# One fp32 product of an LSTM pipeline with 7 block products for 8, and two residual sums moved to GpSimd

## The chip, the cores and the metric

The kernel runs on one core of a Trainium2 chip. The metric is device time in microseconds (us) of one execution, the median of several runs. PE is the TensorE matmul queue, PEld its weight load, DVE is VectorE, ACT is ScalarE, POOL is GpSimd, SP is SyncE.

## What is computed

A batch of 16 sequences, 512 steps, width 512: an LSTM with a residual sum, then a plain tanh RNN over its result with another residual sum. All is fp32.

```python
def step(carry, xw_t):                      # LSTM; xW = x @ Wx0 + b0, Wx0 is 512 x 2048
    prev_h, prev_c = carry
    a = xw_t + prev_h @ Wh
    i, f, o = (sigmoid(a[:, j*512:(j+1)*512]) for j in range(3))
    g = tanh(a[:, 1536:])
    next_c = f * prev_c + i * g
    next_h = o * jnp.tanh(next_c)
...
def step(h, xw_t):                          # RNN; xW = y0 @ Wx1 + b1, Wx1 is 512 x 512
    h_next = jnp.tanh(h @ Wh + xw_t)
...
x = x + LSTM(x)      # y0
x = x + RNN(x)       # y1
```

## The kernel before

**Layout.** Features lie on the 128 partitions. A width of 512 is four slices k. An output column block of 32 features goes to one quarter q of the PE array, so every product is issued as groups of four matmuls (`tiles`, L175), one for each quarter, that run side by side; the small matrix of states or inputs (32 columns) is the loaded one, the weights stream through. The LSTM's 2048 gate columns are 512 columns for each quarter, cut in two halves of 256, each with the four gates of half of the features.

**The input product** x*Wx0 is taken for two steps at once (PAIR, 2 x 16 batch rows). `input0(p, half)` (L191) issues two of the four slices: two groups of four fp32 matmuls with 512 columns, into `in0_ps`. ScalarE writes the bias there first (`bias0`, L468) and later copies the sum, one half after the other, into the banks of the recurrent product (`seed0`, L480), with a mask that picks the rows of the step. `rec0_ps` has two banks for each of the two halves, by the parity of the step.

**The recurrent product** `recurrent0(t)` (L206) adds h*Wh0 with h and Wh0 each in two fp16 parts: 64 matmuls with 256 columns, half 0 first. Its first matmul waits for `h0_ready[0]`, the third slice for `h0_ready[1]`.

**The cell.** VectorE turns the half (`turn0`, L350), adds the two partial sums (`add0`), ScalarE takes the tanh of the gates, VectorE does `gate_products`, `cell`, `state_high` (two instructions, L381 and L382) and `state_low` (L389, which posts `h0_ready`). `add_y0` (L392) and `add_y1` (L420) are the residual sums. Step t of the LSTM and step s = t - 4 of the RNN share an iteration (`turn1`, `add1`, `state1_high`, `state1_low`).

**Order.** Every engine's queue is written out by hand, one loop over t for each engine. PE's order in an iteration: recurrent0(t), half an input0, half an input1 (y0*Wx1, fp32, 128 columns), recurrent1(s). VectorE's order stands in L428 to L461, ScalarE's in L537 to L565. GpSimd has only memsets, an iota and the two maxima over the partitions (L170) by which the weights are scaled. The maximum for the RNN's weights is asked for in iteration 1 and read by VectorE in iteration 2 (`split_rnn_weights`).

## Time and profile before

| | before |
|---|---|
| median of 3 runs | 2290.19 us (2289.34 to 2290.5) |
| the profiled execution's own time | 2287.48 us |
| its span | 2285.6 us |
| PE busy | 2242.9 us, 98% |
| DVE busy | 1974.7 us, 86% |
| ACT busy | 1642.1 us, 72% |
| POOL busy | 1.8 us |
| TensorE clock | granted 0.998 of full |

The trace's timeline gives the start and length of each instruction; neighbours on one engine overlap by their pipelines, so what counts is the distance from start to start. In brackets stands the idle time of the engine ahead of the row and what ended it.

### The profile page before, as it was taken

What the parts mean: (1) busy time and instruction counts of PE and PEld (TensorE: products, weight loads), DVE (VectorE), ACT (ScalarE), POOL (GpSimd) and SP (SyncE); (2) the same over time, 40 slices, a digit from 0 to 9 for tenths busy, and PEclk for the clock granted to TensorE, in tenths of its full rate; (3) what the DMA queues carried; (4) which work ended last, traced back from release to release, by engine and by line L of the source; (5) the groups of instructions that cost most, each with busy time, mean ns of one, the idle gap of its engine ahead of it and who ended that gap; (6) DMA issues with size and microseconds to landing.
All of it is one profiled execution on the core that took longest, in us unless ns stands there. A gap on an engine that the chain in (4) does not pass through costs nothing.

```text
span 2285.6 us, 150617 instructions
## 1 busy us (share of the span) xinstructions
PE 2242.9 (98%) x65564; PEld 1617.4 (71%) x65564; DVE 1974.7 (86%) x10283; ACT 1642.1 (72%) x5662; POOL 1.8 (0%) x10
## 2 busy tenths in 40 slices
PE   5999999999999999999999999999999999999997
PEld 2677777777777777777777777777777777777775
DVE  6888888888888888888888888888888888888887
ACT  5777777777777777777777777777777777777775
POOL 0000000000000000000000000000000000000000
PEclk9999999999999999999999999999999999999999
DMA  5000000000000000000000000000000000000000
GB/s 209 9 23 18 23 18 23 13 18 23 23 18 20 16 18 23 22 19 13 18 23 23 18 23 13 18 23 23 18 13 18 23 23 18 23 14 18 23 13 13
DMA packets 16738, 54.03 MB, mean 24 GB/s; under 512 B 2256, under 2 KB 2384, under 8 KB 14800
## 3 DMA queue, kind: packets, MB, share of 16 engines
q1 hardware_dynamic: 16080, 44.41, 5.5%
q8 instruction: 517, 8.47, 1.5%
q14 instruction: 141, 1.16, 0.2%
HBM read 27.62 MB, written 16.78 MB: 19 GB/s over the span
## 4 chain that ended last, share of the span: by engine, by line
PE 97%; DVE 2%; ACT 1%; issue 1%; POOL 0%; DVEq 0%; ACTq 0%; POOLq 0%
PE rec_ps L178 39%; PE in_ps L178 38%; PE rnn_ps L178 20%; ACT wh_part L478 1%; DVE largest_slice L277 0%; DVE turned L353 0%; DVE wh_part L321 0%; DVE uv L365 0%; DVE h_parts L381 0%; DVE pre_sb L359 0%; ACT gates_cell L502 0%; DVE h_parts L389 0%; ACT wx_sb L466 0%; DVE turned L403 0%; ACT rnn_ps L498 0%
## 5 line engine op out<-in xcount | busy, mean ns | idle before, releaser
L178 PE MATMUL in_ps<-wx_sb,x_sb 128*32 128x512 f32 x8192 | 977.4, 594 | 22.4 <-ACT wx_sb L466 22.4
L178 PE MATMUL rec_ps<-wh_part,h_parts 128*32 128x256 f16 x32704 | 988.9, 273 | 4.4 <-DVE h_parts L389 4.4
L178 PEld LDWEIGHTS rec_ps<-wh_part,h_parts 128*32 128x32 f16 x32704 | 867.5, 97 | 12.1 <-issue 7.0
L353 DVE STREAM_TRANSPOSE turned<-rec_ps 128x256 f32<-128x256 f32 x1024 | 460.4, 450 | 201.2 <-PE rec_ps L178 155.7
L178 PEld LDWEIGHTS in_ps<-wx_sb,x_sb 128*32 128x32 f32 x8192 | 258.9, 110 | 332.1 <-issue 318.9
L178 PEld LDWEIGHTS rnn_ps<-wx_sb,y 128*32 128x32 f32 x8192 | 247.0, 110 | 302.6 <-issue 301.1
L488 ACT ACTIVATE rec_ps<-in_ps,mask_scaled 128x256 f32<-128x256 f32 x1022 | 405.8, 434 | 2.0 <-PE in_ps L178 1.6
L178 PE MATMUL rnn_ps<-wh_part,h_parts 128*32 128x128 f16 x16352 | 323.4, 219 | 7.9 <-DVE h_parts L417 7.9
L178 PE MATMUL rnn_ps<-wx_sb,y 128*32 128x128 f32 x8192 | 318.4, 273 | 1.3 <-ACT rnn_ps L498 1.3
L502 ACT ACTIVATE gates_cell<-gate_ps,unscale 128x128 f32<-128x128 f32 x511 | 187.5, 367 | 181.2 <-DVE gate_ps L359 181.2
L498 ACT ACTIVATE rnn_ps<-rnn_ps,mask_scaled 128x128 f32<-128x128 f32 x511 | 174.8, 342 | 188.4 <-DVE turned L403 188.1
L178 PEld LDWEIGHTS rnn_ps<-wh_part,h_parts 128*32 128x32 f16 x16352 | 287.6, 97 | 9.2 <-ACT rnn_ps L498 5.5
L502 ACT ACTIVATE gates_cell<-pre_sb,unscale 128x128 f32<-128x128 f32 x511 | 205.3, 402 | 120.6 <-DVE pre_sb L359 120.5
L507 ACT ACTIVATE o_scaled<-gates_cell 128x32 f32<-128x32 f32 x1024 | 226.5, 221 | 16.1
L365 DVE SCALAR_TENSOR_TENSOR uv<-gates_cell 128x64 f32<-128x64 f32 x1024 | 227.2, 222 | 1.8 <-ACT gates_cell L502 1.3
L370 DVE SCALAR_TENSOR_TENSOR gates_cell<-uv 128x32 f32<-128x32 f32 x1024 | 196.8, 192 | 35.1
L389 DVE TENSOR_TENSOR h_parts<-h_full,h_parts 128x32 f16<-128x32 f32 x1024 | 192.0, 187 | 18.9
L512 ACT ACTIVATE tanh_c_sb<-gates_cell 128x32 f32<-128x32 f32 x512 | 117.6, 230 | 106.8 <-DVE gates_cell L370 106.7
L549 ACT ACTIVATE h_full<-pre,unscale 128x64 f32<-128x64 f32 x511 | 172.2, 337 | 2.3 <-DVE pre L407 2.3
L403 DVE STREAM_TRANSPOSE turned<-rnn_ps 128x128 f32<-128x128 f32 x512 | 162.0, 316 | 12.4 <-PE rnn_ps L178 3.2
L359 DVE TENSOR_TENSOR gate_ps<-turned 128x128 f32<-128x128 f32 x512 | 153.5, 300 | 17.6
L469 ACT ACTIVATE in_ps<-b_sb 128x512 f32<-128x512 f32 x256 | 150.9, 590 | 0.1
(52 smaller groups left out, 1272.9 us busy)
## 6 DMA issues: line engine op xcount, KB each, us to landing
x_sb<-xT SPq DMA_DIRECT2D x32, 512.0 KB, 3.7
yT<-y SPq DMA_DIRECT2D x64, 256.0 KB, 2.0
wh_sb<-wh SPq DMA_DIRECT2D x5, 1024.0 KB, 9.6
wx_sb<-wx SPq DMA_DIRECT2D x5, 1024.0 KB, 18.1
b_sb<-b SPq DMA_DIRECT2D x1, 256.0 KB, 2.7
b_sb<-b SPq DMA_DIRECT2D x1, 64.0 KB, 12.2
h_first<-h0T SPq DMA_DIRECT2D x1, 32.0 KB, 19.9
```

The source lines that it names most:

```text
L178: last = nc.tensor.matmul(out[QUAD * q:QUAD * (q + 1)], states, weights(q), start=False, stop=True, tile_position=(0, QUAD * q), skip_grou ...
L353: nc.vector.transpose(turned0[:, half].rearrange("p b n -> p (b n)"), rec0_ps[t % 2][half][:, 0:COLSH]).then_inc(turned0_done[half], 1)
L359: nc.vector.tensor_tensor(slices(pre0[half]), turned0[:, half, :, 0:BATCH], turned0[:, half, :, BATCH:], ALU.add).then_inc(pre0_done[half], 1)
L365: nc.vector.scalar_tensor_tensor(uv[:, half], gates_cell[:, half, 0:2], 1.0, gates_cell[:, half, 3:5], ALU.add, ALU.mult).then_inc(uv_done ...
L370: nc.vector.scalar_tensor_tensor(gates_cell[:, half, GATES], uv[:, half, 1], 0.5, uv[:, half, 0], ALU.mult, ALU.add).then_inc(cell_done[ha ...
L389: nc.vector.tensor_tensor(h0_parts[:, subs, BATCH:], slices(h0_full[:, cols]), h0_parts[:, subs, 0:BATCH], ALU.subtract).then_inc(h0_ready ...
L403: nc.vector.transpose(turned1[:, :].rearrange("p b n -> p (b n)"), rec1_ps).then_inc(turned1_done, 1)
L488: last = nc.scalar.activation(rec0_ps[t % 2][half][:, 0:COLSH], in0_ps[t // PAIR % 2][:, half * COLSH:(half + 1) * COLSH], ACT.Copy, scale ...
L498: nc.scalar.activation(rec1_ps, in1_ps[s // PAIR % 2], ACT.Copy, scale=own).then_inc(seed1_done, 1)
L502: nc.scalar.activation(gates_cell[:, half, 0:GATES].rearrange("p g n -> p (g n)"), pre0[half], ACT.Tanh, scale=unscale[0][:, :] if t else ...
L507: nc.scalar.activation(o_scaled[:, half], gates_cell[:, half, 2], ACT.Copy, bias=H_SCALE / 2, scale=H_SCALE / 2).then_inc(o_scaled_done[ha ...
L549: nc.scalar.activation(h1_full[:, :], pre1[:, :], ACT.Tanh, scale=unscale[1][:, :] if s > 1 else 1.0).then_inc(h1_full_done, 1)
```

## The change

Four steps (SPAN) of x*Wx0 are taken together as a 2 x 2 block product: rows are the first and second pair of steps, the inner dimension is cut in two (slices 0,1 and 2,3), the columns are the halves. With Strassen's way in Winograd's form 7 block products do for 8. A "unit" is one group of four matmuls with 128 columns; a step has 7 units, written as groups with 256 or 128 columns (`units`). The sums that it needs:

- of x: four sums of 256 elements a partition for each 16 steps (`sum_x`, GpSimd), and of Wx0 four sums of 2048 elements a partition once, at the start (`sum_wx0`, GpSimd), and one of the bias;
- of the products: `c11`, `c12`, `z` and `v` are accumulated in PSUM. In each span of four steps ScalarE writes two biases (`bias_z`, `bias_v`), starts c11 from z (`begin_c11`) and copies v to SBUF (`copy_v`), one of these four in each iteration, in place of one `bias0` in every second iteration; VectorE adds z and v twice (`begin_c12`, `finish_c22`), in two iterations of four, ahead of `turn0(0, t)`.

To have a bank for c11 and c12, the second half of the recurrent product has one bank in place of two (`rec0_second_ps`), so `seed0` is cut in two: the seed of half 1 is written for the coming step at the top of the iteration, that of half 0 a step ahead as before.

`add_y0` and `add_y1` go from VectorE to GpSimd. `add_y0` becomes two instructions there, since h0_full has to be scaled first (`h0_true`). The next step's `state_high(0)` on VectorE waits for `h0_unscaled`, and the tanh of the RNN on ScalarE for `y1_done`.

```diff
+            for i in range(4):
+                sum_x(0, i)
+            reduce_largest(0)
+            for i in range(4):
+                sum_wx0(i)
...
+            for t in range(END):
+                s = t - LAG
+                if s >= 1:
+                    add_y1(s - 1)
+                if t < STEPS:
+                    add_y0(t)
+                if t == 1:
+                    reduce_largest(1)
+                v, c = divmod(t, CHUNK)
+                if 3 <= c < 7 and v + 1 < CHUNKS:
+                    sum_x(v + 1, c - 3)
...
+            def add_y0(t):
...
+                for half in range(HALVES):
+                    pool.wait_ge(h0_full_done[half], t + 1)
+                if t:
+                    pool.wait_ge(y0_done, t)
+                nc.gpsimd.tensor_scalar(h0_true[:, :], h0_full[:, :], 1.0 / H_SCALE, None, ALU.mult).then_inc(h0_unscaled, 1)
+                pool.wait_ge(h0_unscaled, t + 1)
+                nc.gpsimd.tensor_tensor(y0[:, t // PAIR % Y0_PAIRS, :, t % PAIR], slices(h0_true[:, :]),
+                                        x_sb[:, v % 2, :, t % CHUNK], ALU.add).then_inc(y0_done, 1)
...
+            def units(g, first, end):
+
+                z = z_ps[g % 2]
+                products = (
+                    (z, lambda k: x_pair(g, 0, k), wx0_block(0, 0)),
+                    (v_ps[g % 2], lambda k: x_sum(g, 0, k), wx0_sum(0)),
+                    (z, lambda k: x_sum(g, 1, k), wx0_sum(1)),
+                    (c11_ps, lambda k: x_pair(g, 0, SUBH + k), wx0_block(1, 0)),
+                    (z, lambda k: x_sum(g, 2, k), wx0_sum(2)),
+                    (c12_ps, lambda k: x_sum(g, 3, k), wx0_block(1, 1)),
+                    (z, lambda k: x_pair(g, 1, SUBH + k), wx0_sum(3)),
+                )
...
+            def begin_c12(g, t):
+
+                dve.wait_ge(slot_done, slots_until(t - 1))
+                dve.wait_ge(v_copied, g)
+                dve.wait_ge(seed0_done[1], t + 1)
+                nc.vector.tensor_tensor(c12_ps, z_ps[g % 2], v_sb[:, :], ALU.add).then_inc(c12_begun, 1)
...
                 dve.wait_ge(tanh_c_done[half], n)
+                if n > 1:
+                    dve.wait_ge(h0_unscaled, n - 1)
...
                         dve.wait_ge(cell_zeroed, 1)
+                    g, part = divmod(t + 5, SPAN)
+                    if t < SLOTS:
+                        if part == 2:
+                            begin_c12(g, t)
+                        elif part == 3:
+                            finish_c22(g, t)
                     turn0(0, t)
...
-                if rnn_state:
-                    add_y1(s - 1)
...
-                if lstm:
-                    add_y0(t)
...
-                if t + 1 < STEPS:
-                    seed0(t + 1)
+                if t < STEPS:
+                    act.wait_ge(slot_done, slots_until(t - 1))
+                    g, part = divmod(t + 5, SPAN)
+                    ahead = t < SLOTS
+                    seed0(1, t)
+                    if ahead and part == 2:
+                        copy_v(g)
+                    if t + 1 < STEPS:
+                        seed0(0, t + 1)
+                    if part == 0 and g < SPANS:
+                        act.wait_ge(seed0_done[0], t + 2)
+                        bias_z(g).then_inc(z_biased, 1)
+                    elif part == 1 and ahead:
+                        act.wait_ge(seed0_done[0], t + 2)
+                        begin_c11(g).then_inc(c11_begun, 1)
+                    elif part == 3 and g + 1 < SPANS:
+                        bias_v(g + 1).then_inc(v_biased, 1)
```

PE, one iteration of the steady part, before (`in_ps` is the input product of the LSTM, `rec_ps` its recurrent product, `rnn_ps<-wx_sb,y` and `rnn_ps<-wh_part,h_parts` those of the RNN):

```order
L178 MATMUL rec_ps<-wh_part,h_parts 32x256 x64
L178 MATMUL in_ps<-wx_sb,x_sb 32x512 x8
L178 MATMUL rnn_ps<-wx_sb,y 32x128 x8
L178 MATMUL rnn_ps<-wh_part,h_parts 32x128 x32
L178 MATMUL rec_ps<-wh_part,h_parts 32x256 x64
```

and PE in the changed kernel, one iteration and the start of the next (`wx_sums` and `x_sums` are the sums of Wx0 and of x, `c_ps` holds c11 and c12):

```order
L272 MATMUL rec_first_ps<-wh_part,h_parts 32x256 x32
L272 MATMUL rec_second_ps<-wh_part,h_parts 32x256 x32
L272 MATMUL in_ps<-wx_sums,x_sums 32x128 x4
L272 MATMUL in_ps<-wx_sums,x_sums 32x256 x8
L272 MATMUL c_ps<-wx_sb,x_sb 32x256 x4
L272 MATMUL rnn_ps<-wx_sb,y 32x128 x8
L272 MATMUL rnn_ps<-wh_part,h_parts 32x128 x32
L272 MATMUL rec_first_ps<-wh_part,h_parts 32x256 x32
```

The input product of an iteration has 8 x 512 columns before and 4 x 128 + 12 x 256 after, seven eighths; nothing else on PE moved.

VectorE from the end of the cell to the next turn, before:

```order
L381 TENSOR_TENSOR h_parts<-o_scaled,gate_ps 128x2x16
L382 TENSOR_TENSOR h_full<-o_scaled,gate_ps 128x32
L425 TENSOR_TENSOR y<-y,h_full 128x4x16
L389 TENSOR_TENSOR h_parts<-h_full,h_parts 128x2x16
L381 TENSOR_TENSOR h_parts<-o_scaled,tanh_c_sb 128x2x16
L382 TENSOR_TENSOR h_full<-o_scaled,tanh_c_sb 128x32
L389 TENSOR_TENSOR h_parts<-h_full,h_parts 128x2x16
L403 STREAM_TRANSPOSE turned<-rnn_ps 128x128
L397 SCALAR_TENSOR_TENSOR y<-h_full,x_sb 128x4x16
L407 TENSOR_TENSOR pre<-turned 128x64
L353 STREAM_TRANSPOSE turned<-rec_ps 128x256
```

and in the changed kernel, ahead of an iteration with `begin_c12`:

```order
L547 TENSOR_TENSOR h_parts<-o_scaled,gate_ps 128x2x16 [waits h0_unscaled,tanh_c_done_0,o_scaled_done_0]
L548 TENSOR_TENSOR h_full<-o_scaled,gate_ps 128x32
L555 TENSOR_TENSOR h_parts<-h_full,h_parts 128x2x16 [waits h0_full_done_0]
L547 TENSOR_TENSOR h_parts<-o_scaled,tanh_c_sb 128x2x16 [waits h0_unscaled,tanh_c_done_1,o_scaled_done_1]
L548 TENSOR_TENSOR h_full<-o_scaled,tanh_c_sb 128x32
L555 TENSOR_TENSOR h_parts<-h_full,h_parts 128x2x16 [waits h0_full_done_1]
L561 STREAM_TRANSPOSE turned<-rnn_ps 128x128 [waits rec1_done]
L565 TENSOR_TENSOR pre<-turned 128x64 [waits turned1_done]
L517 TENSOR_TENSOR c_ps<-in_ps,v_sb 128x256 [waits seed0_done_1,v_copied,slot_done]
L503 STREAM_TRANSPOSE turned<-rec_first_ps 128x256 [waits rec0_done_0]
```

The two residual sums are gone from this queue, and the addition of 256 elements stands between `add1` and `turn0(0)`.

GpSimd's queue of the changed kernel, at the first maximum over the partitions (`largest_all`), and then from iteration 0 to iteration 2. An ISA row stands where the rows behind it need another program on GpSimd; `x_sums` and `wx_sums` are the sums of x and of Wx0, `h_true` and `y` belong to `add_y0`:

```order
L208 TENSOR_TENSOR x_sums<-x_sb,x_sums 128x256 [waits x_summed]
L192 ISA
L192 ISA largest_all<-largest 128x1 [waits largest_done]
L219 ISA
L219 TENSOR_TENSOR wx_sums<-wx_sb 128x2048 [waits wx0_doubled]
...
L243 TENSOR_TENSOR y<-h_true,x_sb 128x4x16 [waits h0_unscaled]
L192 ISA
L192 ISA largest_all<-largest 128x1 [waits largest_done]
L241 ISA
L241 TENSOR_SCALAR h_true<-h_full 128x64 [waits y0_done,h0_full_done_1,h0_full_done_0]
```

The kernel before has such a row ahead of the iota and one ahead of the first maximum, two in all; the changed one has five: ahead of the iota, of each maximum, and of what follows each maximum.

## Rows read from the trace of the kernel before

**Rows 1.** The page, parts 1 and 4: busy time, and the chain that ended last.

```profile
PE 2242.9 (98%) x65564; PEld 1617.4 (71%) x65564; DVE 1974.7 (86%) x10283; ACT 1642.1 (72%) x5662; POOL 1.8 (0%) x10
PE 97%; DVE 2%; ACT 1%; issue 1%; POOL 0%; DVEq 0%; ACTq 0%; POOLq 0%
```

**Rows 2.** Timeline, PE: one iteration. Columns: start, length, what ran, number of instructions.

```profile
1000.73 1.93 PE L178 MATMUL rec_ps<-wh_part,h_parts 128*32 128x256 f16 x64
1002.47 1.90 PE L178 MATMUL in_ps<-wx_sb,x_sb 128*32 128x512 f32 x16
1004.19 0.62 PE L178 MATMUL rnn_ps<-wx_sb,y 128*32 128x128 f32 x16
1004.63 0.63 PE L178 MATMUL rnn_ps<-wh_part,h_parts 128*32 128x128 f16 x32
1005.07 1.93 PE L178 MATMUL rec_ps<-wh_part,h_parts 128*32 128x256 f16 x64
```

**Rows 3.** Windows: from iteration 5 to 509 (length, busy time of each engine).

```profile
65.04:2258.78 2193.74, 2193.71 (x64512) 1589.82 (x64516) 1915.88 (x10081) 1597.55 (x5545) 0.00 (x0) 1.00 0.06 19
```

**Rows 4.** Timeline, DVE: the same iteration as rows 2.

```profile
1001.83 0.45 DVE L353 STREAM_TRANSPOSE turned<-rec_ps 128x256 f32<-128x256 f32 x1 [0.30 <-PE rec_ps L178]
1002.32 0.30 DVE L359 TENSOR_TENSOR gate_ps<-turned 128x128 f32<-128x128 f32 x1
1002.71 0.45 DVE L353 STREAM_TRANSPOSE turned<-rec_ps 128x256 f32<-128x256 f32 x1
...
1004.32 0.18 DVE L381 TENSOR_TENSOR h_parts<-o_scaled,gate_ps 128x32 f16<-128x32 f32 x1
...
1004.65 0.18 DVE L389 TENSOR_TENSOR h_parts<-h_full,h_parts 128x32 f16<-128x32 f32 x1
...
1005.10 0.19 DVE L389 TENSOR_TENSOR h_parts<-h_full,h_parts 128x32 f16<-128x32 f32 x1
...
1005.66 0.23 DVE L407 TENSOR_TENSOR pre<-turned 128x64 f32<-128x64 f32 x1
```

**Rows 5.** Timeline, PE, then DVE: iterations 510 and 511, which have no input product.

```profile
2263.03 1.93 PE L178 MATMUL rec_ps<-wh_part,h_parts 128*32 128x256 f16 x64 [0.31 <-DVE h_parts L389]
...
2267.28 1.93 PE L178 MATMUL rec_ps<-wh_part,h_parts 128*32 128x256 f16 x64 [0.32 <-DVE h_parts L389]
...
2266.95 0.18 DVE L389 TENSOR_TENSOR h_parts<-h_full,h_parts 128x32 f16<-128x32 f32 x1
```

**Rows 6.** Timeline: an iteration in which VectorE was late by itself.

```profile
1013.77 2.12 PE L178 MATMUL rec_ps<-wh_part,h_parts 128*32 128x256 f16 x64
1013.81 0.19 DVE L381 TENSOR_TENSOR h_parts<-o_scaled,tanh_c_sb 128x32 f16<-128x32 f32 x1 [0.29 <-issue]
...
1014.14 0.19 DVE L389 TENSOR_TENSOR h_parts<-h_full,h_parts 128x32 f16<-128x32 f32 x1
...
1014.38 1.21 PEld L178 LDWEIGHTS rec_ps<-wh_part,h_parts 128*32 128x32 f16 x48 [0.28 <-DVE h_parts L389]
```

**Rows 7.** Timeline, ACT: the same iteration as rows 2 and the one before.

```profile
1002.65 0.37 ACT L502 ACTIVATE gates_cell<-gate_ps,unscale 128x128 f32<-128x128 f32 x1 [0.19 <-DVE gate_ps L359]
...
1004.57 0.80 ACT L488 ACTIVATE rec_ps<-in_ps,mask_scaled 128x256 f32<-128x256 f32 x2
1005.72 0.34 ACT L498 ACTIVATE rnn_ps<-rnn_ps,mask_scaled 128x128 f32<-128x128 f32 x1 [0.35 <-DVE turned L403]
```

**Rows 8.** Timeline, POOL: all from the iota on, and VectorE's maximum ahead of the second.

```profile
12.33 0.13 POOL L167 IOTA partition<- 128x1 int32 x1 [10.85 <-issue]
22.27 0.38 POOL L170 PARTITION_ALL_REDUCE largest_all<-largest  x1 [9.81 <-DVE largest L277]
49.80 0.35 POOL L170 PARTITION_ALL_REDUCE largest_all<-largest  x1 [27.15 <-DVE largest L277]
...
49.55 0.15 DVE L277 TENSOR_REDUCE largest<-largest_slice 128x1 f32<-128x4 f32 x1
```

**Rows 9.** Timeline, PE: the recurrent product of iteration 4, near the start.

```profile
59.08 1.93 PE L178 MATMUL rec_ps<-wh_part,h_parts 128*32 128x256 f16 x64 [1.58 <-DVE h_parts L389]
```

More of the change, by code:

```diff
@@ L167, in _, with reduce_largest @@
             nc.gpsimd.iota(partition[:, :], [[0, 1]], 0, 1).then_inc(numbered, 1)
-            for l in range(2):
+            def reduce_largest(l):
                 pool.wait_ge(largest_done, l + 1)
@@ new lines, in first_span @@
+            def first_span():
+                pe.wait_ge(x_in[0], 16)
+                pe.wait_ge(first_biased, 1)
+                for k_half in range(HALVES):
+                    for n, (out, second, half) in enumerate(((c11_ps, 0, 0), (c12_ps, 0, 1), (z_ps[0], 1, 0), (v_ps[0], 1, 1))):
+                        for k in range(SUBH):
+                            if n == 0:
+                                pe.wait_ge(wx0_doubled, k_half * SUBH + k + 1)
+                            tiles(out, x_pair(0, second, k_half * SUBH + k),
+                                  lambda q: wx0_block(k_half, half)(k, q, 0, COLSH))
@@ new lines, in units @@
+            def units(g, first, end):
[9 more added lines that the diff above has]
+                )
+                sum_of = {1: 0, 2: 1, 4: 2, 5: 3}
+                u = first
+                while u < end:
+                    j, (k, n) = u // 4, divmod(u % 4, 2)
+                    if u % 4 == 0:
+                        if j == 0 and g % PER_CHUNK == 0:
+                            pe.wait_ge(x_in[g // PER_CHUNK % 2], loads(g // PER_CHUNK))
+                        if j in sum_of:
+                            sums_ready(g, sum_of[j])
+                    count = 2 if n == 0 and u + 1 < end else 1
+                    lo, hi = n * COLSH // 2, (n + count) * COLSH // 2
+                    out, states, weights = products[j]
+                    last = tiles(out[:, lo:hi], states(k), lambda q: weights(k, q, lo, hi))
+                    u += count
+                last.then_inc(slot_done, 1)
@@ L214, in recurrent0 @@
                         for part in weights:
-                            last = tiles(rec0_ps[t % 2][half][:, 0:COLSH], states[:, k], lambda q: part[:, k, q, cols])
+                            last = tiles(rec0_ps(t, half), states[:, k], lambda q: part[:, k, q, cols])
                     last.then_inc(rec0_done[half], 1)
@@ L236, in _ @@
             begin_banks()
-            for half in range(HALVES):
-                input0(0, half)
+            first_span()
+            units(1, 0, 4)
             for t in range(STEPS + LAG):
@@ L243, in _ @@
                     recurrent0(0, h_first, [wh0_sb])
-                    for half in range(HALVES):
-                        input0(1, half)
+                    pe.wait_ge(seed0_done[0], 2)
+                    pe.wait_ge(c11_begun, 1)
+                    units(1, 4, 2 * UNITS_PER_STEP)
                 elif t < STEPS:
@@ L521, in _ @@
             act.wait_ge(b0_doubled, 1)
-            for p in range(2):
-                bias0(p)
+            for out, cols in ((c11_ps, 0), (c12_ps, COLSH), (z_ps[0], 0)):
+                nc.scalar.activation(out, b0_sb[:, cols:cols + COLSH], ACT.Copy)
+            nc.scalar.activation(v_ps[0], b0_sb[:, COLSH:COLS], ACT.Copy)
+            bias_z(1)
+            act.wait_ge(b0_diff_done, 1)
+            bias_v(1).then_inc(first_biased, 1)
             act.wait_ge(b1_in, 16)
```

172 lines of the change are left out of this document (120 added, 52 removed).

## The prediction, made before the changed kernel ran

> **What bounds the kernel now.** I read the page first: PE is busy for 98% of the span and the chain that ended last runs over PE for 97% [rows 1]. Then the timeline of PE for one iteration: from the start of one recurrent product to the next it is 1005.07 - 1000.73 = 4.34 us, with no idle time in brackets [rows 2]. Over the 504 iterations from 5 to 509 the mean is 2193.74 / 504 = 4.353 us and PE is busy for all of it [rows 3]. So PE sets the pace. The question is how far behind it the next thing lies. That is the recurrence: end of the recurrent product, VectorE's turn, the gates, the cell, the new state, PE again.
>
> The end of the trace answers it. In iterations 510 and 511 the input product is over, so PE has 1.72 us less to do, and yet the distance is 2267.28 - 2263.03 = 4.25 us, with PE idle for 0.31 us ahead of each, released by VectorE's L389, which posts the first half of the state [rows 5]. L389 ends there at 2267.13, 4.10 us into the iteration, and PE starts 0.15 us later. So **the recurrence alone takes 4.25 us**, 0.10 us less than PE takes now. In an iteration of the middle it is the same chain: L389 at 1004.65 ends 4.10 us behind 1000.73 [rows 2, 4].
>
> The second half of the state has some room. In one iteration VectorE was late by itself (0.29 us, "issue"): its second L389 ended at 1014.33, 0.56 us after the recurrent product had begun; weights went on loading at 1014.38 and the product took 2.12 us for 1.93 [rows 6]. In a plain iteration that L389 ends 0.22 us into the product (1005.29 against 1005.07) [rows 2, 4]. It was later by 0.34 us and cost 0.19, so up to about 0.37 us into the product it costs nothing.
>
> **What the change removes on PE.** The input product takes 1004.19 - 1002.47 = 1.72 us for two groups of four matmuls with 512 columns, 0.215 us for each 128 columns [rows 2]. Seven units of 128 are 1.505 us, so 0.215 us go. Smaller groups might cost more for each column, but the RNN's input product, two groups with 128 fp32 columns, takes 1004.63 - 1004.19 = 0.44 us, the same price, so I add nothing. PE alone would then need 4.353 - 0.215 = 4.138 us. That is below the 4.25 of the recurrence, so **only about half of the saving can be had**, and VectorE's chain becomes the bound.
>
> **What it does to the recurrence.** From turn0 of half 1 (1.98 us in) to the first L389 the work is the same. `add_y1` goes out of it, but it stood where L389 waits for the result of L382 in any case: from L381 to L389 it is 1004.65 - 1004.32 = 0.33 us with `add_y1` between, and 1014.14 - 1013.81 = 0.33 us for the other half, without it [rows 4, 6]. I take 0.01 us off (bounds 0 and its whole length, some 0.1). `state_high` gets a third wait, on a GpSimd result that is some 3 us old by then: nothing, since it waits for two already. So a plain iteration is 4.24 us. At that pace the second L389 ends 4.34 + 0.19 - 4.24 = 0.29 us into the product, within its 0.37.
>
> In two iterations of four VectorE adds 256 elements between `add1` and `turn0(0)`. The nearest rows: the addition of 128 elements takes 0.30 us, of 64 elements 0.23, the turn of 256 elements 0.45 [rows 4]; so 0.35 to 0.45 us busy, and an estimated 0.35 to 0.40 from start to start. `add1` starts 0.59 us into the iteration today (1005.66) and 0.66 at the new pace; the addition would run from 0.80 to about 1.18. `turn0(0)` starts at 1.10 today, but has spare time: `add0(0)` starts at 1.59 (1002.32) and has to be followed by the second turn only at 1.98 (1002.71), when PE has finished; an addition of 128 elements keeps the engine for some 0.2 us before the next can start. So 0.08 us of delay fall into 0.18 us of room and cost nothing. If this cover were gone, two iterations of four would lose up to 0.4 us, 0.2 us on the mean.
>
> ScalarE: one activation of 256 columns is 0.36 to 0.43 us. It does one more in each iteration and no longer the 512 columns of bias in every second. It is idle for 0.35 us ahead of the RNN's seed (L498) and for 0.19 ahead of the gates [rows 7], so this fits, and the first gates are not on the chain through half 1. The seed of half 1, written into the only bank, is ready near the start of its iteration and is wanted 0.87 us in: nothing.
>
> **GpSimd.** Three instructions of 64 elements in an iteration, and every 16 iterations four of 256. Its prices are not in the trace; the maxima over the partitions take 0.35 to 0.38 us, and the second starts 0.10 us behind the end of VectorE's result (49.80 against 49.70) [rows 8]. At 0.15 to 0.5 us each the three fit easily in 4.24. They matter by meeting VectorE. `h_true` is released by the same event as VectorE's second L389, the addition of y0 follows at about 0.5 to 0.9 us, where `add1` starts at 0.66, and the addition of y1 at about 1.5 to 1.8, where `add0(0)` starts at 1.59. Bounds for what such a meeting costs VectorE: 0, and the length of the GpSimd instruction. GpSimd starts 0.10 us behind the event [rows 8]; VectorE needs less for its own results (0.33 us from L381 to L389, of which the two instructions fill nearly all) [rows 6], so VectorE should be ahead. I put 0.05 us on the iterations with the extra addition and 0.01 on the plain ones: mean pace 4.27 us.
> The Trainium skill, SBUF — State Buffer, "Who interferes with whom", has the rule against this part: a VectorE instruction with both inputs in SBUF and a GpSimd instruction that reads SBUF exclude each other, and the one that issues second waits for all of the first. No row here can show it, since GpSimd does nothing in the steady part; it is rival B below.
>
> **The start.** GpSimd now has five changes of program for two. The only row that shows one: 10.85 us of "issue" ahead of the iota [rows 8]. The second, ahead of the first maximum, was over within 9.5 us, since the maximum came 0.28 us behind its input, at 22.27. So each is 0 to 9.5 us, and the iota's row speaks for the upper part; I take 8. Then the first maximum comes some 2 us late, the program for the sums is in at about 32 us, four sums of 2048 elements (2 to 5 us each; I take 4) end at about 48, iteration 1 ends on GpSimd at about 51, the second maximum comes at 59 and `add_y0(2)` at 68. `state_high` of iteration 3 waits for that, so iteration 4 starts near 69 us against 59.08 [rows 9]: **+10 us**, with 0 and +20 as its ends (programs at 0 and at 9.5 to 10.85).
> The Trainium skill, GPSIMD Engine Reference, "Instruction dispatch", gives about 6 us for the first call of freshly loaded code. By that figure the start would lose an estimated 4 to 5 us, and the time would be 5 us lower.
>
> **The sum.** 504 x (4.353 - 4.27) = 42 us off, 10 us on: 32 us less. The profiled execution took 2287.48 us with a span of 2285.6, so it would be 2255; the median is 2290.19, and by the same step 2258. The tail is unchanged.
>
> **Rivals.**
> A, the pace is PE's after all: VectorE without two additions answers sooner, 4.14 to 4.17 us. 2290 - 504 x 0.2 + 10 = 2200. The tail's 4.25, with PE idle, speaks against it.
> B, slower: GpSimd's read of `h0_full` or its two additions hold VectorE up, in the second L389, `add1` and `add0(0)`. A hold of 0.2 us on the second L389 puts it 0.49 us into the product, 0.12 over its room: 4.36 us; with `add0(0)` or `add1` held as well 4.40. 504 x 0.047 + 10: 2324 us. It decides against the change from a mean pace of 4.335 on, that is from 0.095 us of holds on the chain in each iteration. For it: three of VectorE's instructions meet one, and the room is 0.08 to 0.18. Against: VectorE is released first.
> C, no gain to speak of: pace 4.31 by milder holds, and 18 us for the start. 2290 - 22 + 18 = 2286.
>
> **How the numbers follow.** Forecast (2235 to 2276) 0.63, A 0.07, B 0.17, C 0.13. The range leaves out A and the upper part of B: 2222 to 2305. The low end is pace 4.23 and 3 us at the start, rounded down; the high end is pace 4.35 with 16 at the start. Faster by over 0.2% (4.6 us, about what a measurement of this kernel can tell from none): forecast, A and a third of C, 0.75. Within 0.2%: 0.08. Slower: 0.17.
>
> **What would show it.** PE idle ahead of each recurrent product, released by VectorE's first `h_parts` L555: 0.1 us each, 50 us in all (PE alone would show none: A). The distance of products 4.24 in plain iterations, 4.27 to 4.3 in those with L517 or L524. L555, L565 and L509 no longer than L389, L407 and L359 today (0.19, 0.23, 0.30); longer means B. Iteration 4 at 69 us. The forecast is wrong if a wait of PE ends on `c12_begun` or `c22_done`, or if a GpSimd instruction takes over 1 us.

## The result: 2.5% slower, and the profile after

| | before | changed |
|---|---|---|
| median | 2289.77 us (2288.3 to 2290.5, 4 runs) | 2346.36 us (2344.7 to 2350.23, 4 runs) |
| ratio | | 1.025 (1.0233 to 1.0268) |
| span of the profiled execution | 2285.6 us | 2348.4 us |

The forecast was 2258 us, in a range of 2222 to 2305. The page of the changed kernel, parts 1, 3 and 4 (compare [rows 1]):

```profile
PE 2247.6 (96%) x73748; PEld 1953.3 (83%) x73748; DVE 2006.6 (85%) x9513; ACT 1675.3 (71%) x5919; POOL 633.8 (27%) x1679
...
q8 instruction: 583, 9.55, 1.7%
...
PE 93%; DVE 3%; issue 3%; DMA 1%; ACT 0%; POOL 0%; SPq 0%; POOLq 0%; DVEq 0%; ACTq 0%
```

PE has an eighth less of the input product to do, and yet it is busy for 5 us more, with 3% of the chain on "issue". Windows, from iteration 5 to 509 (compare [rows 3]):

```profile
88.98:2321.32 2232.34, 2194.52 (x72520) 1916.32 (x72511) 1930.45 (x9323) 1628.71 (x5793) 598.69 (x1634) 1.00 0.06 19
```

So the 504 iterations take 2232.34 us for 2193.74: **+39 us**, 4.43 us each for 4.35; and iteration 5 begins at 88.98 for 65.04: **+24 us**. Together they are the 63 us of the two spans; the medians are 57 us apart. The clock is 1.00 in both.

PE's timeline, first a plain iteration, then a piece with a stall (compare [rows 2]):

```profile
1012.37 1.06 PE L272 MATMUL rec_first_ps<-wh_part,h_parts 128*32 128x256 f16 x32
1013.24 1.07 PE L272 MATMUL rec_second_ps<-wh_part,h_parts 128*32 128x256 f16 x32
1014.11 0.62 PE L272 MATMUL c_ps<-wx_sb,x_sb 128*32 128x256 f32 x8
...
1016.62 1.06 PE L272 MATMUL rec_first_ps<-wh_part,h_parts 128*32 128x256 f16 x32
```

```profile
999.26 0.87 PE L272 MATMUL rec_second_ps<-wh_part,h_parts 128*32 128x256 f16 x24
1000.66 0.40 PE L272 MATMUL rec_second_ps<-wh_part,h_parts 128*32 128x256 f16 x6 [0.53 <-issue]
1000.79 0.92 PE L272 MATMUL c_ps<-wx_sb,x_sums 128*32 128x128 f32 x16
```

The plain iteration is 1016.62 - 1012.37 = 4.25 us, as forecast (4.24), although it has the addition for c12. 248 of 500 steady iterations lie between 4.21 and 4.29. The others reach up to 5.8 us, and the second piece shows how: the engine stands for 0.53 us **in the middle of a product**, with its inputs there and nothing to wait for. The list of waits names it:

```profile
PEld rec_first_ps L272 <- issue: 45.6, 62, 12.5
PEld rec_second_ps L272 <- issue: 31.1, 72, 0.8
...
PEld in_ps L272 <- issue: 24.6, 52, 1.0
```

Columns: us in total, times, longest. In the kernel before, the weights of the recurrent product (both halves) show 11.6 us in 18 places, some of it at the start.

**What these stalls are.** Queue 8 of part 3 carries the instructions. PE has 73748 matmuls, as many weight loads and 1796 instructions that only wait, 149292 in all; 149292 / 256 = 583, the number of packets on q8. Before it is 132444 / 256 = 517, and the page of the kernel before says:

```profile
q8 instruction: 517, 8.47, 1.5%
```

So TensorE's instructions come in packets of 256 (16 KB). I numbered the weight loads of each trace and looked at the gaps over 0.3 us between two of them, from 100 to 2200 us. In the changed kernel 173 of 189 lie at one and the same place of the 256, the first instruction of a packet, and make 88 us: 0.18 us an iteration, all that the mean is above 4.25. The engine goes on 1.2 to 1.8 us (median 1.41) after the packet's transfer has ended; the transfer takes 0.88 to 1.6 us.
The Trainium skill, Runtime: NRT & Kernel Launch, "Instruction fetch mechanics", has the blocks of 16 KB with 256 instructions and the next one fetched while the present one runs; it holds that crossing a block is "mostly hidden". The blocks agree with q8; the second part does not agree here, where 88 us stand at their starts.

### The profile page after: what moved, and what is told of

It reads as the page before. It is cut to its first block, busy times and chain, and to the rows that moved or that the text cites. A ratio compares the mean times of both kernels' runs of the same rounds, so it can differ in the third digit from the quotient of the medians.

```text
span 2348.4 us, 170028 instructions
## 1 busy us (share of the span) xinstructions
PE 2247.6 (96%) x73748; PEld 1953.3 (83%) x73748; DVE 2006.6 (85%) x9513; ACT 1675.3 (71%) x5919; POOL 633.8 (27%) x1679
## 4 chain that ended last, share of the span: by engine, by line
PE 93%; DVE 3%; issue 3%; DMA 1%; ACT 0%; POOL 0%; SPq 0%; POOLq 0%; DVEq 0%; ACTq 0%
PE in_ps L272 23%; PE rec_first_ps L272 21%; PE rec_second_ps L272 20%; PE rnn_ps L272 19%; PE c_ps L272 10%; DVE wh_part L471 1%; DMA x_sb<-xT 1%; DVE turned L503 0%; DVE uv L529 0%; ACT wh_part L642 0%; DVE pre_sb L509 0%; DVE gates_cell L534 0%; DVE h_parts L547 0%; DVE h_parts L555 0%; DVE h_parts L575 0%
## 5 line engine op out<-in xcount | busy, mean ns | idle before, releaser
L272 PE MATMUL rec_first_ps<-wh_part,h_parts 128*32 128x256 f16 x16352 | 568.1, 274 | 31.7 <-DVE h_parts L555 24.1
L272 PE MATMUL rec_second_ps<-wh_part,h_parts 128*32 128x256 f16 x16352 | 574.5, 273 | 13.0 <-issue 11.7
L241 POOL TENSOR_SCALAR h_true<-h_full 128x64 f32<-128x64 f32 x512 | 189.1, 369 | 1456.1 <-DVE h_full L548 1448.9
L272 PEld LDWEIGHTS rec_second_ps<-wh_part,h_parts 128*32 128x32 f16 x16352 | 463.1, 97 | 34.2 <-issue 31.1
L272 PEld LDWEIGHTS rec_first_ps<-wh_part,h_parts 128*32 128x32 f16 x16352 | 417.7, 96 | 80.0 <-issue 44.2
L272 PE MATMUL in_ps<-wx_sums,x_sums 128*32 128x128 f32 (+1 forms) x7104 | 425.9, 350 | 5.0 <-issue 4.6
L272 PEld LDWEIGHTS in_ps<-wx_sums,x_sums 128*32 128x32 f32 x7104 | 262.8, 110 | 90.5 <-issue 15.1
L503 DVE STREAM_TRANSPOSE turned<-rec_first_ps 128x256 f32<-128x256 f32 x512 | 229.8, 449 | 97.5 <-PE rec_first_ps L272 96.4
L503 DVE STREAM_TRANSPOSE turned<-rec_second_ps 128x256 f32<-128x256 f32 x512 | 230.3, 450 | 70.0 <-PE rec_second_ps L272 35.1
L272 PE MATMUL c_ps<-wx_sb,x_sb 128*32 128x256 f32 x2096 | 175.8, 383 | 27.7 <-ACT wx_sb L618 25.9
```

What stands on the lines that cost most here:

```text
L241: nc.gpsimd.tensor_scalar(h0_true[:, :], h0_full[:, :], 1.0 / H_SCALE, None, ALU.mult).then_inc(h0_unscaled, 1)
L272: last = nc.tensor.matmul(out[QUAD * q:QUAD * (q + 1)], states, weights(q), start=False, stop=True, tile_position=(0, QUAD * q), skip_grou ...
L503: nc.vector.transpose(turned0[:, half].rearrange("p b n -> p (b n)"), rec0_ps(t, half)).then_inc(turned0_done[half], 1)
```

## The experiments

Each ran beside the kernel before, on the same chip as it. A name with a_ is a variant of the changed kernel, with b_ of the kernel before. "Instructions" are TensorE's in a steady iteration, "mean" is that of iterations 5 to 509 in the profiled execution. The last column is the time in gaps over 0.3 us at packet starts.

| kernel | us | ratio | instructions, of them only waiting | plain iteration | mean | at packet starts |
|---|---|---|---|---|---|---|
| before | 2290 | 1 | 258.5, 2.5 | 4.35 | 4.353 | none to be told |
| b_split | 2313 | 1.011 | 290.5, 2.5 | 4.36 | 4.405 | 20 |
| b_pool | 2295 | 1.003 | 258.5, 2.5 | 4.35 | 4.360 | none to be told |
| b_swap | 2288 | 1.000 | 258.5, 2.5 | 4.35 | 4.351 | none to be told |
| b_fewwaits | 2289 | 1.000 | 256, 0 | 4.35 | 4.351 | none to be told |
| changed | 2346 | 1.025 | 291.5, 3.5 | 4.25 | 4.429 | 88 |
| a_dve | 2357 | 1.029 | 291.5, 3.5 | 4.25 | 4.455 | 80 |
| a_noin1 | 2335 | 1.020 | 260, 4 | 4.25 | 4.402 | 124 |
| a_norec1 | 2264 | 0.989 | 235, 3.5 | 4.25 | 4.261 | none to be told |
| a_rec1 | 2332 | 1.019 | 259.5, 3.5 | 4.25, 4.48 | 4.388 | 7 |
| a_lock60 | 2312 | 1.010 | 256, 0 | 4.17, 4.48 | 4.346 | 0 |
| a_lock150 | 2310 | 1.010 | 256, 0 | 4.17, 4.48 | 4.345 | 0 |
| a_pooladd | 2303 | 1.007 | 256, 0 | 4.25 | 4.327 | 0 |
| a_start | 2292 | 1.001 | 256, 0 | 4.25 | 4.327 | 0 |
| a_mix | 2288 | 0.999 | 256, 0 | 4.17 | 4.315 | 0 |
| a_mix_split | 2295 | 1.003 | 288, 0 | 4.17 | 4.334 | 8 |
| a_mix2 | 2262 | 0.988 | 256, 0 | 4.17 | 4.268 | 0 |
| a_swap | 2331 | 1.019 | 291.5, 3.5 | 4.17 | 4.378 | 96 |
| a_headwait | 2299 | 1.005 | 289, 1 | 4.25 | 4.342 | 44 |
| **a_fewwaits** | **2242** | **0.979** | 288, 0 | 4.17 | 4.236 | 26 |

### Each part of the change alone

`b_split`: the kernel before, with its input product in smaller groups.

```diff
-                    last = tiles(in0_ps[p % 2][:, 0:COLS], x_sb[...],
-                                 lambda q: wx0_sb[:, k, q])
+                    for lo in (0, COLSH):
+                        last = tiles(in0_ps[p % 2][:, lo:lo + COLSH], x_sb[...],
+                                     lambda q: wx0_sb[:, k, q, lo:lo + COLSH])
```

> The kernel before, with each of its 512-column matmuls of the LSTM's input product issued as two with 256 columns: the same columns and the same result, but 144 matmuls and 144 weight loads in an iteration for 128 and 128, as many as the changed kernel has. Theory I (the delivery of TensorE's instructions became the bound): idle times named issue appear inside the recurrent product, the mean pace goes from 4.353 to 4.45-4.55 us, the time to 2340-2390 us. Theory C (GpSimd holds VectorE up): nothing of GpSimd changed, so 2290 us and pace 4.35.

2312.77 us, ratio 1.0106 (1.009 to 1.0122), mean 4.405, less than theory I asked for and more than theory C allows. The stalls appear with nothing but the size of groups changed, 20 us of them at packet starts, and no GpSimd at work. Waits of `b_split`; in the kernel before the row has 11.6 us, 18 times:

```profile
PEld rec_ps L178 <- issue: 26.1, 53, 2.1
```

`b_pool`: the kernel before with `add_y0` and `add_y1` on GpSimd as in the change. `a_dve`: the changed kernel with both back on VectorE.

> The kernel before, with the two residual sums on GpSimd and nothing else changed. Theory C: the holds push the state past its room, pace over 4.40 us from iteration 5 on. Theory I: pace 4.35 as before, since TensorE's instructions are the same; only the start is longer by some 10 to 15 us for GpSimd's changes of program: 2300-2305 us.

> The changed kernel with the two residual sums back on VectorE; GpSimd keeps the sums of x and of Wx0. Theory C: pace 4.25-4.28 us, so some 75 to 90 us less than the changed kernel's 2346. Theory I: the pace stays at 4.41-4.46, and only the start is shorter, by 5 to 10 us: 2336-2345 us.

2294.53 us, ratio 1.0028 (1.0017 to 1.0038), mean 4.360; and 2356.98 us, 1.0294 (1.0268 to 1.0319). The move costs the old kernel 0.007 us an iteration and helps the new one, whose time with the sums back on VectorE is even above the band of theory I. Contention with the residual sums isn't the cause.

`a_noin1`: the changed kernel without the matmuls of `input1`, so that y0*Wx1 is missing from the RNN.

> The changed kernel without the RNN's input product (y0*Wx1 is left out), which takes 16 matmuls and 16 weight loads out of each iteration: 256 instructions as in the kernel before. The recurrence of the LSTM still takes 4.25 us. Theory I: the idle times named issue go, nearly all iterations take 4.25 us, time 2250-2265 us. Theory C: the same pace as the changed kernel, 4.43 us, and 2346 us.

2335.1 us, 1.0202 (1.0185 to 1.0218). Theory I missed. With 260 instructions (the 4 that only wait had not been counted) it still lost 124 us at packet starts, so the number in an iteration can't be all. Of its 141 gaps over 0.4 us there, 56 ended, and the packet began, 2.4 to 2.8 us into the iteration, and none in the first 1.6 us.

### Number, place, or kind

`a_norec1` leaves 60 of the 64 instructions of the RNN's recurrent product out. `a_rec1` keeps the result and joins that product's two fp16 parts of the weights in one operand of 256 columns:

```diff
-                for k in range(SUB):
-                    for part in weights:
-                        last = tiles(rec1_ps, states[:, k], lambda q: part[:, k, q])
+                for k in range(SUB):
+                    last = tiles(rec1_ps, states[:, k], lambda q: wh1_both[:, k, q])
```

`a_lock60` and `a_lock150` are `a_rec1` with each wait of PE on a matmul (the diff of `a_fewwaits` below), 256 instructions an iteration, and 86 or 41 tiny matmuls at the start:

> The changed kernel with 60 of the 64 instructions of the RNN's recurrent product left out of each iteration after the first (the RNN's part of the output is another); 235 TensorE instructions an iteration for 291.5. Theory F (TensorE's instructions arrive in packets of 256; the engine stands when a packet is needed too early): a packet now lasts 4.6 us for 3.9, the stalls named issue go, the pace is 4.25 to 4.28 for 4.43, total 2255 to 2275 us. Rival W (the engine stands for something else that the shorter iteration brings, its waits or its accumulators): stalls as before, 2320 us or more.

> The changed kernel, same result, with the two fp16 parts of the RNN's recurrent weights side by side as one moving operand of 256 columns: the product has 32 instructions for 64, the iteration 259.5 for 291.5; VectorE turns and adds 256 columns for 128 (about +0.2 us an iteration off the path). Theory F: as where the RNN's input product was left out, 260 an iteration and 4.403 us, so a pace of 4.38 to 4.42, 2315 to 2340 us. Rival W: 4.43 or more, since VectorE has more work and nothing else has changed: 2346 to 2380.

> The kernel with the joined parts, its TensorE waits arranged so that each iteration has exactly 256 instructions, and 86 small matmuls at the start that set where in the iteration a packet of 256 begins: after 60 of the 128 instructions of the LSTM's recurrent product (0.8 us from its start). Where the RNN's input product was left out, no stall fell where a packet began there, and 28 of 40 where it began 2.4 us from the start. Theory F: no stalls, a pace of 4.25 to 4.30, 2265 to 2290 us. Rival W, to which the place of a packet is nothing: the pace of the joined kernel, 4.38 to 4.45.

> The same kernel with 41 small matmuls at the start for 86, so that a packet begins after instruction 150 of each iteration, in the products of x, 2.2 to 2.5 us from the start. Theory F: stalls in most iterations, a pace of 4.5 to 4.8, 2390 to 2540 us, over 100 us longer than the kernel with 86, although it has 90 instructions less. Rival W: the same time within 5 us.

`a_norec1`: 2264.25 us, 0.9893 (0.9877 to 0.991): the stalls go with the instructions. `a_rec1`: 2332.18, 1.0191 (1.0176 to 1.0207): in the forecast band, but for another reason: only 7 us were left at packet starts, and a second level of 4.48 us came up. `a_lock60` 2311.63 (1.0086 to 1.0116) and `a_lock150` 2310.47 (1.0082 to 1.0112): no stall in either, and both outside the bands of theory F. **My idea of the place fell.** By the rows the 4.48 is VectorE, which turns and adds 256 columns of the RNN ahead of the turn that PE waits for, in iterations with c12 or c22.

`a_pooladd` and `a_start` gave that addition to GpSimd, and the second also made both maxima ahead of all sums:

> Same result. The kernel with 256 instructions an iteration has no stall left, but two levels: 4.17 us where VectorE has no sum c12 or c22 and 4.48 where it has one, and VectorE stands in neither (turn 0.44 us and four-fold addition 0.60 us of the RNN). Here the addition is two on GpSimd, first the parts (128 elements), then the rows (64), some 0.85 us beside 1.4 to 2.2 us that GpSimd is busy. If VectorE is what bounds the 4.48, the pace is 4.17 to 4.20 everywhere, 2222 to 2240 us, 2 to 3% faster than the kernel before. If it was the wait for c12 or c22 itself, half the iterations stay at 4.4 or more, 2290 to 2311 us. If GpSimd's longer chain makes the RNN's state late, 4.3 to 4.4 everywhere, 2290 to 2320.

> The same, and both maxima across partitions follow each other on GpSimd ahead of every sum (the weights Wh1 are loaded before Wx0 for it): the time between two kinds of GpSimd program (9.4, 6.9, 5.9 and 7.0 us idle in the first 82 us) falls due twice for four times. Start theory: iteration 5 begins 15 to 18 us earlier (2 x 6.5 us of changes and 5 us earlier sums), 2205 to 2222 us. If the sums' hold on VectorE (its fp16 low parts 2776 ns each for 685) is all that counts, 5 us or less.

2303.42 us (1.0053 to 1.0081): by its mean the third case, though 314 of 504 iterations take 4.21 to 4.29 us and the others mostly 4.3 to 4.5. The RNN's tanh on ScalarE waits for GpSimd (316 us in all) and stands ahead of the first gates. 2292.1 us (1.0005 to 1.0022): iteration 5 at 77.75 us for 89.45, 12 us, between the two forecasts.

`a_mix` splits the addition between both engines; `a_mix_split` is `a_mix` with 32 more instructions; `a_mix2` moves four sums of x:

```diff
-                if 3 <= c < 7 and v + 1 < CHUNKS:
-                    sum_x(v + 1, c - 3)
+                if c in X_SUM_STEPS and v + 1 < CHUNKS:      # (2, 3, 6, 7)
+                    sum_x(v + 1, X_SUM_STEPS.index(c))
```

> Same result, with the early maxima. The addition of the RNN's parts is on VectorE in the iterations that precede one without c12 or c22 (4.17 us each when it was so in all), and on GpSimd, now ahead of the sum y0, in the two of four that precede one with c12 or c22. In the kernel with all of them on GpSimd the RNN's tanh waited 0.64 us for GpSimd and pushed the first gates' tanh from 1005.05 to 1005.23. Theory V (VectorE bounds one half, ScalarE's order behind GpSimd the other): 4.17 in one half and 4.2 to 4.3 in the other, mean 4.19 to 4.25, 2225 to 2255 us. Rival: GpSimd's instructions hold VectorE's two-input ones wherever they fall (0.45 us for 0.30 us for the addition of the gates), 4.30 or more, 2280 to 2295 us.

> The same kernel, with each matmul of 256 columns of the RNN's recurrent product as two of 128: the same columns and the same data, 288 TensorE instructions an iteration for 256, nothing else changed. Theory F (packets of 256 instructions): the stalls come back, 0.10 to 0.20 us an iteration, 50 to 100 us over the kernel without the split. Rival W: within 10 us of it.

> Same result; only the steps at which GpSimd makes the sums of x differ: steps 2, 3, 6 and 7 of 16 for 3 to 6. In the kernel with 3 to 6, two of 16 iterations lasted 4.67 to 4.84 us, and in them VectorE's addition of the second half's gates (two inputs and an output in SBUF) took 0.87 us for 0.29 while GpSimd made a sum of x (0.73 us); the two sums in iterations where GpSimd doesn't also add the RNN's parts fell beside other work and cost nothing. If that coincidence is the price, 65 of 500 iterations lose their 0.5 us each: mean 4.24 to 4.26, 2248 to 2262 us. If GpSimd's total work is what counts, no change, 2284 to 2289.

`a_mix` 2287.73 us, 0.9994 (0.9985 to 1.0003), in the rival's band. In its slowest iterations (66 of 504, 4.7 to 4.8 us) two instructions met, here VectorE and GpSimd:

```profile
1047.40 0.87 DVE L544 TENSOR_TENSOR pre_sb<-turned 128x128 f32<-128x128 f32 x1
```

```profile
1047.39 0.73 POOL L223 TENSOR_TENSOR x_sums<-x_sums,x_sb 128x256 f32<-128x256 f32 x1
```

The same addition takes 0.29 us at 1005.13. `a_mix2`, 2261.81 us, 0.9878 (0.9861 to 0.9894), shows that this meeting was a price: 0.047 us an iteration. It is rival B's mechanism, in a place where the changed kernel doesn't have it. The Trainium skill, SBUF — State Buffer, "Who interferes with whom", has GpSimd and the second port of VectorE under one exclusive lock; these rows agree, 0.58 us lost to an instruction of 0.73.
`a_mix_split`, 2295.43 us (1.002 to 1.0039), lost 0.019 us an iteration where I expected 0.10 to 0.20, of it 8 us in 21 gaps at packet starts. It lies in the rival's band (within 10 us): number alone was too simple.

### The waits

`a_fewwaits` is the changed kernel with the early maxima, the 86 tiny matmuls of `a_lock60` at the start, and on PE no instruction that only waits in the steady part. Waits that another one implies are dropped, the others moved so that no matmul carries two. Its core:

```diff
                 for half in range(HALVES):
-                    pe.wait_ge(seed0_done[half], t + 1)
+                    if half or t < 2 or t > SLOTS:
+                        pe.wait_ge(seed0_done[half], t + 1)
...
-                pe.wait_ge(in1_biased, r + 1)
-                pe.wait_ge(y0_done, PAIR * (r + 1))
+                if r < 2 or r >= PAIRS - 1:
+                    pe.wait_ge(in1_biased, r + 1)
...
+                    if u == 24:
+                        pe.wait_ge(c22_done, g)
+                    if u in (10, 26) and g > 1:
+                        pe.wait_ge(y0_done, SPAN * (g - 1) + (u == 26) * PAIR)
```

> The changed kernel as it was, with 64 instructions of the RNN's recurrent product and no more work on VectorE, and with the early maxima; of TensorE's waits only those are left that an own matmul can carry, so that it has no instruction that only waits: 288 instructions an iteration for 291.5. Theory F by count alone: a packet would last 3.71 us at the pace of 4.17, under the 3.9 at which the changed kernel stood still for it, so stalls of 0.1 to 0.2 an iteration, 4.30 to 4.40, 2265 to 2320 us. Theory E (the instructions that only wait make the next packet's request late, and one stood on the recurrence at the head of the recurrent product): stalls under 0.05, 4.18 to 4.25, 2215 to 2255 us.

**2242.09 us, 0.9787 (0.9768 to 0.9806).** The window of iterations 5 to 509, and a plain iteration with the state ahead of its end:

```profile
78.04:2213.14 2135.10, 2127.05 (x72512) 1793.22 (x72513) 1916.10 (x9326) 1619.91 (x5795) 594.36 (x1635) 1.00 0.06 20
```

```profile
1002.52 1.07 PE L271 MATMUL rec_first_ps<-wh_part,h_parts 128*32 128x256 f16 x32
...
1006.45 0.19 DVE L559 TENSOR_TENSOR h_parts<-h_full,h_parts 128x32 f16<-128x32 f32 x1
1006.70 0.29 PE L271 MATMUL rec_first_ps<-wh_part,h_parts 128*32 128x256 f16 x3
```

PE does the same 72500 matmuls in 2127 us for 2195, with 4.17 us from start to start in most iterations (1002.52 to 1006.70). The product starts 0.06 us behind the end of VectorE's state (1006.64). In the changed kernel it is 0.15, from this row to PE at 1012.37:

```profile
1012.03 0.19 DVE L555 TENSOR_TENSOR h_parts<-h_full,h_parts 128x32 f16<-128x32 f32 x1
```

Over iterations 5 to 509 the medians are 0.054 and 0.146 us, and 461 and 407 of the 504 lie within 0.003 us of them: PE still follows the state at 4.17, only sooner. Three kernels take this apart. `a_swap` and `b_swap` only exchange two waits in the changed kernel and in that of before; `a_headwait` puts one wait back into `a_fewwaits`.

```diff
 a_swap, at the head of recurrent0
+                    if t and half == 0:
+                        pe.wait_ge(h0_ready[0], t)
                     pe.wait_ge(seed0_done[half], t + 1)
...
-                        if t and half == 0 and k % SUBH == 0:
-                            pe.wait_ge(h0_ready[k // SUBH], t)
+                        if t and half == 0 and k == SUBH:
+                            pe.wait_ge(h0_ready[1], t)
 a_headwait, against a_fewwaits
-                    if half or t < 2 or t > SLOTS:
-                        pe.wait_ge(seed0_done[half], t + 1)
+                    pe.wait_ge(seed0_done[half], t + 1)
```

> The changed kernel with two waits ahead of the LSTM's recurrent product in the other order: the wait for the seed (long done) now stands on the instruction that only waits, and the wait for VectorE's low state, the last to be met, on the first matmul. The same 291.5 instructions an iteration. Theory H (that hop costs 0.08 us of each recurrence): plain iterations 4.17 for 4.25, with the stalls as they were a mean of 4.35 to 4.40, 2300 to 2330 us. Theory E in full (a wait on an own instruction also delays the next packet): stalls halved too, 4.25 to 4.32, 2255 to 2290. Rival: neither, 2346.

> The fast kernel of 2242 us with one wait put back: the redundant wait for the seed at the head of the recurrent product, which moves the wait for VectorE's low state onto an instruction of its own. 289 instructions for 288. Theory H: plain iterations 4.25 again, mean 4.30 to 4.33, 2275 to 2290 us. Theory E in full: the stalls of the changed kernel as well, 4.38 to 4.43, 2310 to 2335. Rival, only the count matters: 2242 to 2247.

> The kernel before with the same two waits exchanged. TensorE has little left to gain (98% busy); it waited for VectorE's low state in part of the iterations. Theory H: 0 to 0.03 us an iteration, 2272 to 2290 us. If it came near the fast kernel (2242), the seven products would be worth nothing.

`a_swap`: 2331.37 us (1.0162 to 1.0209), at the upper end of theory H; no level at 4.25 any more, 222 of 504 iterations at 4.20 or less, and the stalls as they were. `a_headwait`: 2298.59 us (1.0035 to 1.0061), between the bands of H and E; not one iteration below 4.21, 328 between 4.21 and 4.29. So the 0.08 us is **the hop from an instruction that only waits to the matmul behind it**. Of two waits the build put the second one written (`h0_ready`) on an instruction of its own, where the recurrence passes through it. The stalls: 44 us with that one wait, 26 without. `b_swap` 2287.96 us, 0.9998 (0.9989 to 1.0006): nothing in the steady part, where PE has other work. But its last two iterations, those of [rows 5], are the clearest proof:

```profile
2262.97 1.95 PE L178 MATMUL rec_ps<-wh_part,h_parts 128*32 128x256 f16 x64 [0.23 <-DVE h_parts L391]
...
2267.16 1.95 PE L178 MATMUL rec_ps<-wh_part,h_parts 128*32 128x256 f16 x64 [0.22 <-DVE h_parts L391]
```

The distance is 4.19 us for 4.25, with two waits exchanged and nothing else. The same two of `a_swap` are 4.17 apart, with PE idle for 0.22 us ahead of each. **So the recurrence takes 4.17 to 4.19 us without the hop**, and it is what the 4.17 of `a_fewwaits` shows.

`b_fewwaits` does to the kernel before what `a_fewwaits` did to the changed one:

> The kernel before with none of TensorE's instructions only waiting (256 an iteration for 258.6), all waits on matmuls; eight products, work and sums as before. TensorE is 98% busy with 4.35 us of matmuls an iteration, so theory T (before is bound by its matmuls): 0 to 0.02 us an iteration, 2278 to 2290 us. Rival: the wait-only instructions cost here as there, 0.1 us an iteration, 2235 to 2245 us, and the seven products brought nothing.

2288.84 us, 1.0002 (0.9993 to 1.0011); PE is busy for 2192.98 of the 2193.08 us of its steady part. **So the waits alone bring nothing: the 2.1% of `a_fewwaits` need the change too.** Its steady part is 97 us shorter than the changed kernel's, its start 11 us, from the early maxima. Since PE is full in `b_fewwaits`, a pace under 4.35 needs less work on PE, which only the seven products give. Whether the residual sums on GpSimd are needed for it too no run separates.

## Why the prediction was wrong

**Right:** what the input product saves and the plain iteration. The forecast's 4.24 us stands in 248 of 500 iterations as 4.25, with `turn0(0)` 1.10 us in (1013.47 behind 1012.37) and the addition for c12 at no cost, as forecast in "What it does to the recurrence" (the 0.03 us added for meetings with GpSimd did not come). The second state there ends 0.29 us into the product, in its room; the prediction has 0.29 too, but by 0.19 where its own reading, 0.22, gives 0.32. PE's idle time of 0.1 us ahead of each product, named as a sign, is not in the rows (2.4 us in 11 places in the steady part); that the state bounds the pace is seen from the constant 0.146 us behind it. Also right: GpSimd holds little. Timeline, DVE of the changed kernel, the same iteration (compare [rows 4]):

```profile
1012.47 0.19 DVE L555 TENSOR_TENSOR h_parts<-h_full,h_parts 128x32 f16<-128x32 f32 x1
...
1012.92 0.23 DVE L565 TENSOR_TENSOR pre<-turned 128x64 f32<-128x64 f32 x1
1013.07 0.42 DVE L517 TENSOR_TENSOR c_ps<-in_ps,v_sb 128x256 f32<-128x256 f32 x1
1013.47 0.45 DVE L503 STREAM_TRANSPOSE turned<-rec_first_ps 128x256 f32<-128x256 f32 x1
1013.96 0.30 DVE L509 TENSOR_TENSOR gate_ps<-turned 128x128 f32<-128x128 f32 x1
```

**Wrong, the step that failed:** "Smaller groups might cost more for each column ... so I add nothing." I priced the 32 more instructions by the columns they stream, and the mean by the plain iteration plus 0.03 us. What was missing is the supply of instructions: 0.18 us an iteration, 90 us in all. The forecast of the pace was 4.27 and it is 4.43, 80 us; from the plain 4.25 to 4.43 it is 90 us, and 88 stand in gaps at packet starts. The row that held the warning was in the page, 517 packets on q8 beside 132444 instructions, one packet in each iteration. The changed kernel needs 1.14 packets in a shorter one.

**Wrong in its frame:** "the recurrence alone takes 4.25 us" [rows 5]. It was read rightly, but 0.06 to 0.08 us of it was the wait's hop. Rival A named the level (4.14 to 4.17) that `a_fewwaits` has, but by luck: it had PE set the pace and VectorE answer sooner without its two additions. In `b_swap` VectorE has them, and the chain still takes 4.19 us.

**Mis-sized, the start:** +24 us for +10. GpSimd and PE at the start of the changed kernel (compare [rows 8, 9]):

```profile
27.07 0.38 POOL L192 PARTITION_ALL_REDUCE largest_all<-largest  x1 [9.18 <-issue]
35.87 5.05 POOL L219 TENSOR_TENSOR wx_sums<-wx_sb 128x2048 f32<-128x2048 f32 x1 [8.42 <-issue]
...
72.94 0.38 POOL L192 PARTITION_ALL_REDUCE largest_all<-largest  x1 [5.71 <-issue]
80.59 0.41 POOL L241 TENSOR_SCALAR h_true<-h_full 128x64 f32<-128x64 f32 x1 [7.27 <-issue]
```

```profile
60.35 1.90 PE L272 MATMUL rec_first_ps<-wh_part,h_parts 128*32 128x256 f16 x32 [12.00 <-DVE h_parts L555]
...
81.78 1.90 PE L272 MATMUL rec_first_ps<-wh_part,h_parts 128*32 128x256 f16 x32 [7.43 <-DVE h_parts L555]
```

The four changes of program are 5.7 to 9.2 us, mean 7.6, as taken (8). The value was right, but its source was luck: the fifth, ahead of the iota, took 0.29 us here for the 10.85 of [rows 8], so that row is no price of a change. Iteration 1 began at 60.35 for 44.50 before, 15.9 us later; I had it done on GpSimd by 51. The first maximum came 4.8 us later (27.07 for 22.27); the other 11 us lie between it and iteration 1, where VectorE makes the low parts of Wh0. Groups by line of before and of the changed kernel:

```profile
L321 DVE SCALAR_TENSOR_TENSOR wh_part<-wh_sb,w_scale,wh_part 128x512 f16<-128x512 f32 x20 | 13.7, 746 | 1.5 <-ACT wh_part L478 1.5
```

```profile
L471 DVE SCALAR_TENSOR_TENSOR wh_part<-wh_sb,w_scale,wh_part 128x512 f16<-128x512 f32 x20 | 31.3, 1629 | 1.3 <-ACT wh_part L642 1.1
```

Those of Wh0 (16 of the 20) ran beside GpSimd's sums of Wx0, and the group was busy for 17.6 us more: rival B again, in the one stretch where I hadn't looked for it. In the first 62 us they took 1815 ns each in the changed kernel and 1814 in `a_dve`, which has the sums but no residual sum on GpSimd, and 752 in `b_pool`, where it is the reverse. So it is the sums. `b_pool` has its first maximum at 17.44, for 22.27 before, and its iteration 5 begins only 2 us later than before, with both later changes in it. The second maximum and the change behind it, 72.94 to 80.59, add 7 us ahead of iteration 4: it began at 81.78 for 59.08, and the forecast was 69.

**The rivals and the range:** B's number was nearest (2324), its cause in the steady part was not this one: `b_pool` leaves it 0.007 us an iteration and `a_dve` nothing. The low end of the range doesn't follow from its terms: a pace of 4.23 and 3 us at the start give 2231, not 2222. My own "would make it wrong" (a wait on c12 or c22, GpSimd over 1 us) did not come to pass in the steady part; the forecast fell to something that was not on the list.

**Open:** what, beside the number, makes a packet late. `a_noin1` (260 instructions, 4 only waiting) lost 124 us at packet starts, `a_rec1` (259.5 and 3.5) 7, `a_fewwaits` (288 and none) 26. In `a_noin1` the transfer of the next packet began 2.2 to 2.7 us (medians) after the engine had come to the end of one packet, where that fell 1.6 to 3.2 us into the iteration, and 0.5 to 1.2 us after where it fell in the first 1.2 us. What holds the request back there no run tells.

## What to carry to other kernels

Count TensorE's instructions for each microsecond, not only its columns: here the kernel before, with a packet of 256 for each 4.3 us, shows no stall, and the changed one, with one for each 3.9, lost 4%. The count is a warning and no rule: `a_noin1` lost more at one for each 4.3 us, `a_fewwaits` only 1% at one for each 3.8. Where a queue recurs through a semaphore, put the wait that is met last on the matmul itself, and see that the one met early is the one on its own instruction; then a change that shortens the other work can pay. When a profile says "issue" in mid-product, compare the places modulo 256 before looking for contention.

## What the runs showed of the hardware that was not expected

- TensorE's instructions arrive by DMA in packets of 16 KB; a late one stops the engine until 1.2 to 1.8 us after the transfer's end (88 us in the changed kernel, none seen in those with 256 an iteration and no wait-only instruction).
- A wait on an instruction of its own costs 0.06 to 0.08 us on the chain (4.25 for 4.17 us in `a_headwait` and `a_swap`, 4.25 for 4.19 in the last iterations of `b_swap`).
- A sum of 256 elements on GpSimd (0.73 us) holds a VectorE addition with two SBUF inputs for 0.58 us (0.87 for 0.29), and long ones make VectorE's low parts 1629 ns for 746.
